# Layer 0 scan: the rows of step sizes, B and C projected half a channel set at a time, in two slots

## The chip, the cores and the metric

The kernel runs on one core of one Trainium2 chip. The metric is the device time of one execution in microseconds (us); lower is better. The kernel is one program for a network of four layers; the change is in the selective scan of layer 0.

## The reference, cut to what matters

Layer 0 takes x of shape (4, 48, 48, 128), normalises it, projects it to 256 channels, convolves it 3x3 and applies silu. The result (xc) is scanned in four directions k: by rows, by columns, and both backwards (L = 2304 positions, d = 256 channels, N = 16 states, R = 8 ranks of the step size):

```python
xs = jnp.stack([x0, x1, x0[..., ::-1], x1[..., ::-1]], axis=1)
x_dbl = jnp.einsum('bkdl,kcd->bkcl', xs, x_proj_w)
dts_r, Bs, Cs = (x_dbl[:, :, :R], x_dbl[:, :, R:R + N], x_dbl[:, :, R + N:])
dts = jnp.einsum('bkrl,kdr->bkdl', dts_r, dt_proj_w)
dt = jax.nn.softplus(dts + dt_proj_b[None, :, :, None])
A = -jnp.exp(A_logs).reshape(K, d, N)
def step(h, inp):
    dt_l, u_l, B_l, C_l = inp
    dA = jnp.exp(dt_l[..., None] * A)
    h = h * dA + (dt_l * u_l)[..., None] * B_l[:, :, None, :]
    y = jnp.einsum('bkdn,bkn->bkd', h, C_l)
    return (h, y)
```

`x_dbl` are the "rows": 8 rows of step sizes, 16 of B and 16 of C for each position, 40 in all, each a sum over the 256 channels. Then come a skip term, a norm, a gate and an output projection, and layers 1 to 3 (deformable convolution, linear attention and experts, causal attention and spectral filters), which the change doesn't touch.

## The kernel before, in words

Layer 0 works image by image (a loop of 4). For each image, the scan is cut into 24 chunks g: four directions k = g // 6, six chunks of 384 positions each (RC = 384). Each chunk has 16 slots, one for each state n; the 384 slots of an image are numbered s, so s = 16 g + n. The 256 channels lie in two halves h of 128 partitions. Everything is fp32.

What a slot s does, on five engines that each follow an order written out in the program and meet at semaphores:

- ScalarE makes `decays(s)` (L500): exp(dt * A), one activation for each half, two slots ahead.
- The input dt * u * B comes into PSUM through `make_input(s)` on TensorE. For the states in TURNED (1, 2, 3, 6, 8, 11, 13, 14) ScalarE scales the turned dt * u by B (`turned_input`, L490, three activations, four slots ahead) and TensorE turns it back (L406, six matmuls). For the others VectorE makes a diagonal matrix of B (`diagonal`, L556, two slots ahead) and TensorE multiplies by it (L408, twelve matmul records).
- VectorE scans: `scan(s)` (L579), one instruction over both halves.
- GpSimd carries the last state of the chunk before into a decay buffer (`carry`, L636) and multiplies the states by C (L649, `hC`). The rows of C come there by DMA: SP stores them to a DRAM scratch (`store_C`, L341) and loads each one spread over all partitions (L352).
- TensorE adds the 16 states up in PSUM: `sum_states(s)` (L419, six matmuls), three slots behind.

Next to this, the next chunk's step sizes are prepared ("project"), each piece in a slot of its own: TensorE makes the rows (`rows`, L361) in slot 0, ScalarE copies them from PSUM (`copy_rows`, L460) in slot 1, TensorE projects the step size of half 0 (`delta`, L377) in slot 2, ScalarE makes a softplus of it (`softplus`, L470, L472, L474) in slot 3, VectorE finishes it (`delta`, L549) in slot 4; half 1 follows in slots 5 to 7; then B is turned and copied (slots 8, 9), and dt * u is turned and copied (slots 10 to 13).

At a chunk's end the sum y goes to SBUF. While k is 0 or 1 (forward), ScalarE copies it in slot 3 of the next chunk (`keep_y`, L506); while k is 2 or 3 (backward), VectorE adds it in slot 2 of the next chunk, behind the scan (`add_y`, L586). Both wait for `sum_states` of the old chunk's last state, and `sum_states` of the new chunk's state 0, in slot 3, waits for them.

TensorE's order in a slot is this:

```python
for s in range(NSTEP):
    if s + 1 < NSTEP:
        make_input(s + 1)
    if s >= 3:
        sum_states(s - 3)
    if s // NS + 1 < NCH:
        project(s // NS + 1, s % NS)
```

`rows(g)` is two matmuls, one for each half of the channels, summed in PSUM (`start` at h = 0, `stop` at h = 1); each shows as two records in the trace. Their moving operand is `inputs(g, h)`: for k even a slice of xc with 384 adjacent elements; for k odd the same image read by columns, with a stride.

Of the kernel before, what the change touches and what calls it, by code (L numbers as in the profile page):

```python
# [62 lines left out]
DI, NS, RK, KD = 256, 16, 8, 4  # L63
RC = 384
NRC = L // RC
# [11 lines left out]
def layer0(nc, x_in, w, x_out, c_rows):  # L77
    with ExitStack() as ctx:
        def sb(name, shape, dt=F32):
            return ctx.enter_context(nc.sbuf_tensor("l0_" + name, shape, dt))  # L80
# [3 lines left out]
        ps = w["psum"]  # L84
# [3 lines left out]
        xp_w = sb("xp_w", [P, KD, 2, RK + 2 * NS])  # L88
# [21 lines left out]
        def cut(at, n):  # L110
# [26 lines left out]
        s_id, s_rows, s_lo, s_dtp, s_btp, s_bt, s_sf, s_dt, s_du, s_tp, s_tc = (scan_sem(n) for n in (  # L137
            "ident_laid", "rows_made", "rows_copied", "dt_projected", "B_turned", "B_copied", "softplus_step", "dt_made",
            "dtu_made", "dtu_turned", "dtu_copied"))
# [12 lines left out]
        with nc.Block() as block:  # L152
# [5 lines left out]
            @block.sync  # L158
            def _(sp):
                sp.dma_start(gnx[:], x_in[:, 0:L]).then_inc(s_x, 16)  # L160
                for dst, src in loads:
                    sp.dma_start(dst, src).then_inc(s_w, 16)
# [23 lines left out]
        with nc.Fori(0, NB) as b:  # L186
# [107 lines left out]
            with nc.Block() as block:  # L294

                def chunk(g):

                    k, j = g // NRC, g % NRC
                    col = (NRC - 1 - j) * RC if k >= 2 else j * RC
                    return k, slice(col, col + RC)  # L300

                def inputs(g, h):

                    k, cs = chunk(g)
                    if k % 2 == 0:
                        return xc[:, h, cs]
                    return xc[:, h, :].rearrange("p (y x) -> p x y", y=HH)[:, cs.start // HH:cs.stop // HH, :]
# [6 lines left out]
                work = 7 * BANK  # L314

                def delta_ps(g, h):

                    o = work if g else 2 * BANK * h
                    return ps[:, o:o + RC]

                def turned_dtu_ps(g):

                    return work if g else 4 * BANK
                x2_ps = [ps[:, 2 * BANK * r + X2_AT:2 * BANK * r + X2_AT + RX] for r in range(2)]

                def half(h):

                    return slice(2 + h * (RC + 2), 2 + h * (RC + 2) + RC)
# [24 lines left out]

                @block.tensor
                def _(pe):
                    def rows(g):
                        if g:
                            pe.wait_ge(s_tc, 2 * g)
                        k = g // NRC
                        for h in range(2):  # L360
                            mm = pe.matmul(ps[0:RK + 2 * NS, work:work + RC], xp_w[:, k, h, :], inputs(g, h), start=(h == 0), stop=(h == 1))  # L361
                        mm.then_inc(s_rows, 1)

                    def turn_B(g):
                        if g:
                            pe.wait_ge(s_dt, 2 * g + 2)
                        for t in range(LB):
                            o = work + RC + t * NS
                            mm = pe.transpose(ps[:, o:o + NS], low[0:NS, g % 2, t * P:(t + 1) * P], ident[0:NS, 0:NS])
                        mm.then_inc(s_btp, 1)  # L370

                    def delta(g, h):
                        if h and g:
                            pe.wait_ge(s_dt, 2 * g + 1)
                        else:
                            pe.wait_ge(s_lo, g + 1)
                        pe.matmul(delta_ps(g, h), dtp_w[32:33 + RK, g // NRC, h * P:(h + 1) * P], low[32:33 + RK, g % 2, :],  # L377
                                  start=True, stop=True).then_inc(s_dtp, 1)

                    def turn_dtu(g, part):  # L380
                        if part and g:
                            pe.wait_ge(s_tc, 2 * g + 1)
                        else:
                            pe.wait_ge(s_bt, g + 1)
                            pe.wait_ge(s_du, g + 1)
                        for t in ((0, 1), (2,))[part]:
                            for h in range(2):
                                o = turned_dtu_ps(g) + (t % 2 if g else t) * DI + h * P
                                mm = pe.transpose(ps[:, o:o + P], dtu[:, g % 2, h, t * P:(t + 1) * P], ident[:])
                        mm.then_inc(s_tp, 1)  # L390

                    def make_input(s):
                        n, g = s % NS, s // NS
                        if n == 0:
                            pe.wait_ge(s_tc, 2 * g + 2)
                        if n in TURNED:
                            pe.wait_ge(s_xT, rank[s] + 1)
                        else:
                            pe.wait_ge(s_dg, rank[s] + 1)
                        if s >= 2:  # L400
                            pe.wait_ge(s_scan, s - 1)
                        for h in range(2):
                            for t in range(LB):
                                o = 2 * BANK * (s % 2) + X2_AT + half(h).start + t * P
                                if n in TURNED:
                                    mm = pe.transpose(ps[:, o:o + P], xT[:, rank[s] % 3, t, h * P:(h + 1) * P], ident[:])  # L406
                                else:
                                    mm = pe.matmul(ps[:, o:o + P], dtuT[:, g % 2, t, h * P:(h + 1) * P], diagB[:, rank[s] % 3, t, :],  # L408
                                                   start=True, stop=True)
                        mm.then_inc(s_x2, 1)  # L410

                    def sum_states(s):
                        n, g = s % NS, s // NS
                        pe.wait_ge(s_hc, s + 1)
                        if n == 0 and g:
                            pe.wait_ge(s_ye, g)
                        for t in range(LB):
                            for h in range(2):
                                mm = pe.matmul(y_ps[:, t, h * P:(h + 1) * P], hC[:, s % NHC, h, t * P:(t + 1) * P], ident[:],  # L419
                                               start=(n == 0 and h == 0 and t % 2 == 0), stop=(n == NS - 1), is_transpose=True,  # L420
                                               skip_group_check=True)
                        mm.then_inc(s_y, 1)

                    def project(g, slot):
                        if slot == 0:
                            rows(g)
                        elif slot == 2:
                            delta(g, 0)
                        elif slot == 5:
                            delta(g, 1)  # L430
                        elif slot == 8:
                            turn_B(g)
                        elif slot == 10:
                            turn_dtu(g, 0)
                        elif slot == 12:
                            turn_dtu(g, 1)

                    pe.transpose(ident_ps, ident[:], ident[:]).then_inc(s_id, 1)
                    for slot in range(NS):
                        project(0, slot)  # L440
                    make_input(0)
# [7 lines that stand above are left out]
                    for s in range(NSTEP - 3, NSTEP):  # L449
                        sum_states(s)  # L450

                @block.scalar
                def _(act):
# [52 lines left out]
                        act.activation(yT[:, k, cs.start // P:cs.stop // P, :], y_ps, ACT.Copy).then_inc(s_ye, 1)  # L506

                    def project(g, slot):
                        if slot == 1:
                            copy_rows(g)  # L510
                        elif slot == 3:
                            softplus(g, 0)
                        elif slot == 6:
                            softplus(g, 1)
                        elif slot == 9:
                            copy_B(g)
                        elif slot == 11:
                            copy_dtu(g, 0)
                        elif slot == 13:
                            copy_dtu(g, 1)  # L520
# [12 lines left out]
                    for s in range(NSTEP):  # L533
                        if s + 2 < NSTEP:
                            decays(s + 2)
                        g = s // NS - 1
# [2310 lines left out]
```

## Time and profile before

| | |
|---|---|
| median of 3 runs | 7457.38 us (7455.82 to 7466.65) |
| the profiled execution, its own time | 7461.88 us |
| its span, first to last instruction | 7459.9 us |
| TensorE matmul (PE) busy | 6818.0 us, 91% |
| TensorE weight load (PEld) busy | 5835.0 us, 78% |
| VectorE (DVE) busy | 6015.2 us, 81% |
| ScalarE (ACT) busy | 4738.0 us, 64% |
| GpSimd (POOL) busy | 4602.9 us, 62% |
| scan instructions (L579) | 1536, 1747 ns each |

The span runs from the first to the last instruction; the execution's own time lies around it. Busy shares are means over the whole program. The scan loops of layer 0 are four stretches, one for each image; in the profile's times the second lies between 1040 us and about 1850 us. The timeline merges adjacent instructions of one kind into a row with their count; a bracket at its end gives the idle time of the engine before the row and what ended it. A row without a bracket follows with no idle time worth naming. The time from one row's start to the next row's start is the better measure of what a group of matmuls takes, since the ends of matmuls are modelled and overlap the next.

### The profile page before, as it was taken

What the parts mean: (1) busy time and instruction counts of PE and PEld (TensorE: products, weight loads), DVE (VectorE), ACT (ScalarE), POOL (GpSimd) and SP (SyncE); (2) the same over time, 40 slices, a digit from 0 to 9 for tenths busy, and PEclk for the clock granted to TensorE, in tenths of its full rate; (3) what the DMA queues carried; (4) which work ended last, traced back from release to release, by engine and by line L of the source; (5) the groups of instructions that cost most, each with busy time, mean ns of one, the idle gap of its engine ahead of it and who ended that gap; (6) DMA issues with size and microseconds to landing.
All of it is one profiled execution on the core that took longest, in us unless ns stands there. A gap on an engine that the chain in (4) does not pass through costs nothing. (4 is left out here: it accounts for less than half of the span.)

```text
span 7459.9 us, 178001 instructions
## 1 busy us (share of the span) xinstructions
PE 6818.0 (91%) x63622; PEld 5835.0 (78%) x63622; DVE 6015.2 (81%) x8957; ACT 4738.0 (64%) x10021; POOL 4602.9 (62%) x5010
## 2 busy tenths in 40 slices
PE   8999989999899998999957999888878989989899
PEld 6888768888588885888836878645657989989898
DVE  7999879999799997999945777546667878878787
ACT  6998769997599985999811433216545545545455
POOL 5998749998399882998917766321213545545454
PEclk9999999999899999999969999989999999999999
DMA  2333213332133331333347776300003434444443
GB/s 65 96 96 94 87 53 95 96 96 87 53 96 96 95 88 52 97 95 96 94 132 234 232 203 191 96 6 18 18 19 102 142 119 135 135 126 141 120 138 120
DMA packets 595169, 775.01 MB, mean 104 GB/s; under 512 B 52215, under 2 KB 528408, under 8 KB 592193
## 3 DMA queue, kind: packets, MB, share of 16 engines
q1 hardware_dynamic: 542529, 594.11, 27.1%
q0 software_dynamic: 51840, 169.91, 7.9%
q8 instruction: 542, 8.88, 0.5%
q14 instruction: 258, 2.11, 0.1%
HBM read 730.16 MB, written 33.66 MB: 102 GB/s over the span
## 5 line engine op out<-in xcount | busy, mean ns | idle before, releaser
L579 DVE TENSOR_TENSOR_SCAN l_arena<-l_arena,psum 128x772 f32<-128x772 f32 x1536 | 2641.6, 1747 | 163.3 <-POOL l_arena L649 60.9
L649 POOL TENSOR_TENSOR l_arena<-l_arena 128x768 f32<-128x768 f32 x1536 | 2590.6, 1687 | 4.2 <-issue 1.6
L500 ACT ACTIVATE l_arena<-l_arena,l_A 128x384 f32<-128x384 f32 x3072 | 1668.2, 603 | 16.2 <-DVE l_arena L579 14.0
L408 PE MATMUL psum<-l_arena 128*128 128x128 f32 x9216 | 1213.5, 282 | 102.5 <-DVE l_arena L579 87.7
L408 PEld LDWEIGHTS psum<-l_arena 128*128 128x128 f32 x9216 | 1091.4, 192 | 272.8 <-issue 221.2
L419 PE MATMUL psum<-l_ident,l_arena 128*128 128x128 f32 x9216 | 1255.4, 273 | 4.6 <-POOL l_arena L649 4.6
L419 PEld LDWEIGHTS psum<-l_ident,l_arena 128*128 128x128 f32 x9216 | 1056.7, 142 | 5.6 <-POOL l_arena L649 5.5
L490 ACT ACTIVATE l_arena<-l_arena,l_BT 128x256 f32<-128x256 f32 x2304 | 994.2, 496 | 7.5
L2683 POOL TENSOR_TENSOR st_U<-st_Uc,st_U 128x384 f16<-128x384 f32 x512 | 478.9, 935 | 783.3 <-ACT st_U L2650 783.3
L1211 POOL DMA_INDIRECT l_G<-neighbours,l_idx x648 | 622.3, 960 | 391.0 <-issue 189.8
L406 PE MATMUL psum<-l_ident,l_arena 128*128 128x128 f32 x4608 | 638.7, 275 | 3.6 <-DVE l_arena L579 2.4
L406 PEld LDWEIGHTS psum<-l_ident,l_arena 128*128 128x128 f32 x4608 | 520.0, 142 | 106.6 <-issue 94.3
L2475 PE MATMUL psum<-st_FS,st_xt 128*128 128x128 f16 x6912 | 518.9, 219 | 9.0 <-DMA st_FS<-filter_sums 8.5
L2500 PE MATMUL psum<-st_U,st_W 128*128 128x128 f16 (+3 forms) x6144 | 509.8, 226 | 11.4 <-ACT st_U L2650 9.6
L1054 DVE TENSOR_TENSOR l_G<-l_G,psum 128x1536 f32<-128x1536 f32 (+1 forms) x144 | 366.3, 2547 | 124.7 <-DMA l_G<-neighbours,l_idx 124.2
L2475 PEld LDWEIGHTS psum<-st_FS,st_xt 128*128 128x128 f16 x6912 | 421.1, 97 | 9.9 <-DMA st_FS<-filter_sums 9.3
L2465 PE MATMUL psum<-st_F,st_xt 128*128 128x128 f16 x4608 | 427.7, 219 | 0.0
L2500 PEld LDWEIGHTS psum<-st_U,st_W 128*128 128x128 f16 x6144 | 403.2, 97 | 14.0 <-ACT st_U L2650 10.5
L556 DVE TENSOR_TENSOR l_arena<-psum,l_BT 128x384 f32<-128x384 f32 x768 | 411.3, 536 | 0.0
L2650 ACT ACTIVATE st_U<-st_Uc 128x384 f16<-128x384 f32 x512 | 266.6, 521 | 223.3 <-DVE st_Uc L2607 211.8
L636 POOL COPY l_arena<-l_arena 128x2 f32<-128x2 f32 x1280 | 240.5, 188 | 243.0 <-DVE l_arena L579 151.4
L1259 PE MATMUL psum<-l_ident,l_G 128*128 128x128 f32 x2592 | 319.6, 284 | 66.5 <-DVE l_G L1054 38.9
(469 smaller groups left out, 11778.4 us busy)
## 6 DMA issues: line engine op xcount, KB each, us to landing
l_arena<-c_rows SPq DMA_DIRECT2D x1536, 192.0 KB, 3.0
st_FS<-filter_sums SPq DMA_DIRECT2D x128, 1155.0 KB, 9.5
st_F<-filter_parts SPq DMA_DIRECT2D x128, 320.5 KB, 7.0
neighbours<-l_xt SPq DMA_DIRECT2D x256, 72.0 KB
st_mab<-in_st_mp SPq DMA_DIRECT2D x68, 256.0 KB, 9.5
st_mab<-in_st_mm SPq DMA_DIRECT2D x68, 256.0 KB, 6.9
l_G<-neighbours,l_idx POOLq DMA_INDIRECT x648
l_arena<-in_x SPq DMA_DIRECT2D x4, 1152.0 KB, 5.3
```

The lines of the kernel that those rows point to most:

```text
L406: mm = pe.transpose(ps[:, o:o + P], xT[:, rank[s] % 3, t, h * P:(h + 1) * P], ident[:])
L408: mm = pe.matmul(ps[:, o:o + P], dtuT[:, g % 2, t, h * P:(h + 1) * P], diagB[:, rank[s] % 3, t, :], start=True, stop=True)
L419: mm = pe.matmul(y_ps[:, t, h * P:(h + 1) * P], hC[:, s % NHC, h, t * P:(t + 1) * P], ident[:], start=(n == 0 and h == 0 and t % 2 == 0), ...
L490: ins = act.activation(xT[:, i % 3, t, :], dtuT[:, g % 2, t, :], ACT.Copy, scale=BT[:, g % 2, t, n:n + 1])
L500: act.activation(decay[:, s % NDC, half(h)], dtv[:, g % 2, h, :], ACT.Exp, scale=A[:, g // NRC, h, n:n + 1]).then_inc(s_exp, 1)
L579: dve.tensor_tensor_scan(hbuf[:, n, run], decay[:, s % NDC, run], x2_ps[s % 2][:, run], 0.0, ALU.mult, ALU.add).then_inc(s_scan, 1)
L649: pool.tensor_tensor(hC[:, s % NHC], halves(hbuf[:, s % NS, :]), Cs[:, s % NCS, :].unsqueeze(1).broadcast_to([P, 2, RC]), ALU.mult).then_i ...
L1211: pool.indirect_dma_start(out=G[:, g, 4 * k:4 * k + 4, :].rearrange("p q c -> p (q c)"), out_offset=None, in_=tables[b], in_offset=bass.In ...
L2465: mm = pe.matmul(ps[:, LOW + i * P:LOW + (i + 1) * P], xt[:, xpart, blk, :], tap[:, r, fpart, z, shift + at:shift + at + P], start=(n + m ...
L2475: mm = pe.matmul(ps[:, at + i * P:at + (i + 1) * P], xt[:, xpart, x0 + LB - 1 - i, :], FS[:, r, fpart, z, three, shift + i * P:shift + (i ...
L2500: mm = pe.matmul(ps[:, o:o + hi - lo], W16[:, r, wpart, z, m, :], U16[:, c, upart, lo - c * RC:hi - c * RC], start=False, stop=False, skip ...
L2683: pool.tensor_tensor(U16[:, c, 1, :], src, U16[:, c, 0, :], ALU.subtract).then_inc(s_ul, 1)
```

## The change

The two matmuls of `rows` are no longer issued together in slot 0. Half h = 0 stays in slot 0, half h = 1 goes to slot 1, and the semaphore that tells of the rows is raised by the second. The copy on ScalarE goes from slot 1 to slot 2. The wait ahead of the rows stays with half 0. Everything else is as it was. For the first chunk of an image, which is projected before the loop, the order of the matmuls is unchanged.

```diff
-                    def rows(g):
-                        if g:
+                    def rows(g, h):
+                        if h == 0 and g:
                             pe.wait_ge(s_tc, 2 * g)
-                        k = g // NRC
-                        for h in range(2):
-                            mm = pe.matmul(ps[0:RK + 2 * NS, work:work + RC], xp_w[:, k, h, :], inputs(g, h), start=(h == 0), stop=(h == 1))
-                        mm.then_inc(s_rows, 1)
+                        mm = pe.matmul(ps[0:RK + 2 * NS, work:work + RC], xp_w[:, g // NRC, h, :], inputs(g, h), start=(h == 0), stop=(h == 1))
+                        if h == 1:
+                            mm.then_inc(s_rows, 1)
...
                     def project(g, slot):
-                        if slot == 0:
-                            rows(g)
+                        if slot < 2:
+                            rows(g, slot)
                         elif slot == 2:
                             delta(g, 0)
...
                     def project(g, slot):
-                        if slot == 1:
+                        if slot == 2:
                             copy_rows(g)
                         elif slot == 3:
                             softplus(g, 0)
```

TensorE's order around slot 0 of a chunk, before: the rows (L361, both halves) stand between the sums of slot 0 and the input of scan 2 (L406).

```order
L408 MATMUL psum<-l_arena 128x128 x6
L419 MATMUL psum<-l_ident,l_arena 128x128 x6
L406 MATMUL psum<-l_ident,l_arena 128x128 x6
L419 MATMUL psum<-l_ident,l_arena 128x128 x6
L361 MATMUL psum<-l_xc,l_xp_w 40x384 x2
L406 MATMUL psum<-l_ident,l_arena 128x128 x6
L419 MATMUL psum<-l_ident,l_arena 128x128 x6
L406 MATMUL psum<-l_ident,l_arena 128x128 x6
L419 MATMUL psum<-l_ident,l_arena 128x128 x6
L377 MATMUL psum<-l_arena,l_dtp_w 128x384
L408 MATMUL psum<-l_arena 128x128 x6
```

The same place with the change, where lines from L361 on have moved up by one or two (L405 is the old L406, L407 the old L408, L418 the old L419, L376 the old L377):

```order
L407 MATMUL psum<-l_arena 128x128 x6
L418 MATMUL psum<-l_ident,l_arena 128x128 x6
L405 MATMUL psum<-l_ident,l_arena 128x128 x6
L418 MATMUL psum<-l_ident,l_arena 128x128 x6
L359 MATMUL psum<-l_xc,l_xp_w 40x384
L405 MATMUL psum<-l_ident,l_arena 128x128 x6
L418 MATMUL psum<-l_ident,l_arena 128x128 x6
L359 MATMUL psum<-l_xc,l_xp_w 40x384
L405 MATMUL psum<-l_ident,l_arena 128x128 x6
L418 MATMUL psum<-l_ident,l_arena 128x128 x6
L376 MATMUL psum<-l_arena,l_dtp_w 128x384
L407 MATMUL psum<-l_arena 128x128 x6
```

The second half of the rows now stands behind the input of scan 2 and the sums of slot 1; the delta and the input of scan 4 stand behind both halves, as before.

ScalarE's order in slots 1 to 3, before: the copy (L460) stands ahead of the decays of scan 4 (L500 x2).

```order
L500 ACTIVATE l_arena<-l_arena,l_A 128x384 x4
L460 ACTIVATE l_arena<-psum 40x384
L500 ACTIVATE l_arena<-l_arena,l_A 128x384 x2
L490 ACTIVATE l_arena<-l_arena,l_BT 128x256 x3
L500 ACTIVATE l_arena<-l_arena,l_A 128x384 x2
L506 ACTIVATE l_yT<-psum 128x768
L470 ACTIVATE l_arena<-psum 128x384
```

With the change:

```order
L499 ACTIVATE l_arena<-l_arena,l_A 128x384 x6
L459 ACTIVATE l_arena<-psum 40x384
L489 ACTIVATE l_arena<-l_arena,l_BT 128x256 x3
L499 ACTIVATE l_arena<-l_arena,l_A 128x384 x2
L505 ACTIVATE l_yT<-psum 128x768
L469 ACTIVATE l_arena<-psum 128x384
```

The copy (now L459) stands behind one more pair of decays, which has joined the four ahead of it, and in front of the same turned input, decays, copy of y and softplus.

## Rows read from the trace of the kernel before

**Rows 1.** Busy time of each engine in the second image's scan loop.

```profile
1075.00:1850.00 775.00, 748.04 (x5884) 652.61 (x5884) 730.80 (x614) 695.25 (x1503) 699.91 (x780) 1.00 0.33 94
```

**Rows 2.** Waits, whole run: waiting engine, line, releaser; us, times, longest.

```profile
ACT l_arena L460 <- PE psum L361: 145.2, 92, 2.2
```

**Rows 3.** Timeline of TensorE, a forward chunk with strided rows: start us, us.

```profile
1305.67 0.82 PE L406 MATMUL psum<-l_ident,l_arena 128*128 128x128 f32 x6
1306.33 0.82 PE L419 MATMUL psum<-l_ident,l_arena 128*128 128x128 f32 x6
1307.07 2.75 PE L361 MATMUL psum<-l_xc,l_xp_w 128*40 128x384 f32 x4
1309.75 0.87 PE L406 MATMUL psum<-l_ident,l_arena 128*128 128x128 f32 x6
1310.46 0.82 PE L419 MATMUL psum<-l_ident,l_arena 128*128 128x128 f32 x6
1311.12 0.82 PE L406 MATMUL psum<-l_ident,l_arena 128*128 128x128 f32 x6
1311.77 0.82 PE L419 MATMUL psum<-l_ident,l_arena 128*128 128x128 f32 x6
1312.52 0.91 PE L377 MATMUL psum<-l_arena,l_dtp_w 9*128 9x384 f32 x2
1313.36 1.60 PE L408 MATMUL psum<-l_arena 128*128 128x128 f32 x12
1314.80 0.82 PE L419 MATMUL psum<-l_ident,l_arena 128*128 128x128 f32 x6
```

**Rows 4.** Timeline of TensorE's weight loads, the same chunk, L361.

```profile
1307.72 0.13 PEld L361 LDWEIGHTS psum<-l_xc,l_xp_w 128*40 128x40 f32 x1 [0.49 <-issue]
1308.36 0.13 PEld L361 LDWEIGHTS psum<-l_xc,l_xp_w 128*40 128x40 f32 x1 [0.51 <-issue]
```

**Rows 5.** Timeline of VectorE, the same chunk, scans 0 and 1, 2, 4.

```profile
1305.38 3.41 DVE L579 TENSOR_TENSOR_SCAN l_arena<-l_arena,psum 128x772 f32<-128x772 f32 x2 [0.28 <-PE psum L408]
...
1310.83 1.76 DVE L579 TENSOR_TENSOR_SCAN l_arena<-l_arena,psum 128x772 f32<-128x772 f32 x1 [1.58 <-PE psum L406]
...
1315.17 1.76 DVE L579 TENSOR_TENSOR_SCAN l_arena<-l_arena,psum 128x772 f32<-128x772 f32 x1 [0.46 <-PE psum L408]
```

**Rows 6.** Timeline of TensorE, a chunk whose next reads xc in order.

```profile
1105.55 0.82 PE L419 MATMUL psum<-l_ident,l_arena 128*128 128x128 f32 x6
1106.30 1.48 PE L361 MATMUL psum<-l_xc,l_xp_w 128*40 128x384 f32 x4
1107.71 0.88 PE L406 MATMUL psum<-l_ident,l_arena 128*128 128x128 f32 x6
```

**Rows 7.** Timeline of TensorE's weight loads, that chunk, L361.

```profile
1106.65 0.12 PEld L361 LDWEIGHTS psum<-l_xc,l_xp_w 128*40 128x40 f32 x1 [0.21 <-issue]
1106.97 0.12 PEld L361 LDWEIGHTS psum<-l_xc,l_xp_w 128*40 128x40 f32 x1 [0.20 <-issue]
```

**Rows 8.** Timeline of VectorE, that chunk, scan 2.

```profile
1108.79 1.76 DVE L579 TENSOR_TENSOR_SCAN l_arena<-l_arena,psum 128x772 f32<-128x772 f32 x1 [0.32 <-PE psum L406]
```

**Rows 9.** Timeline of all engines, a backward strided chunk.

```profile
1715.91 1.76 DVE L579 TENSOR_TENSOR_SCAN l_arena<-l_arena,psum 128x772 f32<-128x772 f32 x1 [1.58 <-PE psum L406]
...
1716.85 0.82 PE L419 MATMUL psum<-l_ident,l_arena 128*128 128x128 f32 x6
...
1717.71 0.95 DVE L586 TENSOR_TENSOR l_yT<-l_yT,psum 128x768 f32<-128x768 f32 x1
```

**Rows 10.** Timeline of ScalarE, the chunk of rows 3.

```profile
1309.86 0.48 ACT L460 ACTIVATE l_arena<-psum 40x384 f32<-40x384 f32 x1 [2.16 <-PE psum L361]
...
1311.26 1.29 ACT L490 ACTIVATE l_arena<-l_arena,l_BT 128x256 f32<-128x256 f32 x3
...
1313.46 0.80 ACT L506 ACTIVATE l_yT<-psum 128x768 f32<-128x768 f32 x1
```

**Rows 11.** Timeline of SP's queue, the same chunk: the store of C rows.

```profile
1311.52 0.38 SPq L341 DMA_DIRECT2D c_rows<-l_arena  x1
```

## The prediction

> **What bounds the kernel now.** I read the busy time of a stretch first, then the table of waits, then the timeline of TensorE, VectorE and ScalarE around slot 0 of a chunk. In 775 us of the second image every engine is busy nine tenths of the time, TensorE most (748.04 us), then VectorE (730.80 us), at a granted clock of 1.00, its 2.4 GHz level [rows 1]. So no engine has much room, and the question is who waits for whom, slot by slot.
>
> The table of waits makes the edit look good: ScalarE's copy (L460) waited 145.2 us, 92 times, for the rows' matmuls (L361) [rows 2]. VectorE waits too. In the chunk at 1305 us the fp32 rows occupy TensorE from 1307.07 to 1309.75 [rows 3], the next make_input (L406, for scan 2) comes behind them, and VectorE stands still for 1.58 us before scan 2 [rows 5]. This is a chunk whose next chunk reads xc by columns (a strided operand). Where the next chunk reads it in order, the rows take 1.41 us [rows 6] and the idle time is 0.32 us [rows 8]. Of the 23 chunks of an image in which rows are projected, the first has no sums to make in its first slots, so TensorE isn't full there; of the other 22, 12 are strided and 10 in order: 48 and 40 over four images.
>
> The decisive reading is the next step. From 1305.67 to the end of L408 at 1314.96 TensorE's rows have no idle time between them at all: sums, inputs, rows, inputs, sums, delta, input of scan 4 [rows 3]. And scan 4, at 1315.17, waits another 0.46 us for exactly that L408 [rows 5]. Its end plus 0.21 us is the scan's start, as at scan 2 (1310.62 and 1310.83). So in a forward chunk **TensorE's queue holds VectorE at slot 4**, whatever happened at slot 2. In a backward chunk it holds it one place earlier: add_y (L586) starts at 1717.71, 0.04 us after the sum of the chunk before (L419) ends at 1717.67, while VectorE would have been free at about 1717.59, when scan 2 (started 1715.91, 1.68 us to the next start) was over [rows 9].
>
> **The change, part by part.** It adds and removes no instruction, no wait and no DMA. It moves one of the two rows matmuls behind make_input(2) and sum_states(-2), and the copy behind one pair of decays.
>
> *The move itself.* Between slot 0 and slot 4 TensorE executes the same work. L408 of slot 4 stays behind both halves, and so does the sum for which add_y waits. What scan 2 gains is waited for at scan 4, or at add_y. For a strided chunk: the first half takes 2 x 0.645 us (1307.72 to 1308.36 and on, record to record, [rows 4]) and its exit 0.10, so L406 starts at 1307.07 + 1.39 = 1308.46 instead of 1309.75, ends at 1309.33, and scan 2 starts at 1309.54. VectorE was ready at 1309.25, so 0.29 of the 1.58 us stay. Scan 3 needs its L406, which starts no earlier than now (1311.12) and ends at 1311.99; scan 4 needs L408 and can't be before 1315.17. Net: 0.
>
> *Two new edges.* The rows have a weight tile of 40 columns between tiles of 128, and that costs at each end. Six matmuls of L419 take 0.66 us from start to start where L406 follows (1310.46 to 1311.12), and 0.74 where L361 follows (1306.33 to 1307.07): 0.08 to 0.09 to enter. The rows take 2.68 us against 4 x 0.645 = 2.58: 0.10 to leave. The L406 behind them takes 0.71 us to the next start against 0.65 (1311.12 to 1311.77): 0.06 more. That is 0.25 us for one excursion to the rows, strided [rows 3, 4]. In order: 0.75 against 0.66 to enter, 1.41 against 4 x 0.32 = 1.28, and the same 0.06 behind: 0.28 us [rows 6, 7]. Before there was one excursion in a chunk, now there are two. Bounds for the second: from below 0, since a change from L419 to L406 costs nothing (0.66 for six), and not less, since no instruction goes. From above 0.36: the other excursion in these rows, the delta with its 9-row weights, costs 0.09 to 0.10 to enter and 0.20 to leave (0.84 to the next start against 2 x 0.32), and 0.06 for the group behind is added. I take 0.25 and 0.28, because the edges that come into being (L419 to L361, L361 to L406) are those of these rows, in this very place.
>
> A rule of the Trainium skill speaks for the lower bound: "TensorE: Matmul & The Clock Gate", Part 2, step by step, says that the load of the next weights is pulled ahead of matmuls in flight. By it the second excursion would be free and the time unchanged. The trace agrees inside the 128-column groups, and not at the edge to the rows.
>
> *Does the edge reach the end?* Yes: TensorE's stretch is full and VectorE waits at its end, so 0.25 us there is 0.25 us at scan 4 or add_y. Behind that VectorE has no idle time until the next TensorE-bound place, which starts from its own scans; nothing takes it back. In the first chunk of an image TensorE has gaps and I count 0. Sum: 48 x 0.25 + 40 x 0.28 = 12.0 + 11.2 = **23.2 us slower**.
>
> *The copy, one slot later.* The second half ends about 1.55 us later than the rows did (0.10 + 0.71 + 0.74), so the copy starts at 1311.4 instead of 1309.86 and ends at 1311.9. TensorE's delta (L377), which waits for it, comes at 1312.52 + 0.25: 0.9 us to spare. ScalarE does the pair of decays, 1.0 us of the 1.40 between 1309.86 and 1311.26, inside its old wait, so all behind it slips by 1.55 - 1.0 = 0.55 us: keep_y ends at 1314.8 instead of 1314.26, and sum_states(0), which waits for it, is due at 1314.80 + 0.25 = 1315.05 [rows 3, 10]. That is 0.2 us to spare. I cost it at nothing; if the cover is gone, TensorE has until L408 for scan 5. On SP's queue the store of the C rows waits for the copy: issued at 1311.52 now, it would go at about 1311.9 [rows 11]. What it stores is first read a whole chunk of slots later. Free.
>
> The profiled execution took 7461.88 us around its span of 7459.9; with 23.2 it would be 7485.1. Its time is 4.5 us above the median of the three runs, 7457.38, so for the median I say 7457.4 + 23.2 = **7481 us**, 0.31% more.
>
> **The rivals.**
> (a) *The wait at scan 2 is what counts, and it goes: faster.* Place: slot 2 of 88 chunks. Price: 40 x 0.32 + 48 x (1.58 - 0.29) = 12.8 + 61.9 = 74.7 us, 7383 us. For it: VectorE is the engine with the scans, and two idle times name L406. It decides from the point at which TensorE, after the rows, has 0.3 us (in order) or 1.3 us (strided) of slack before slot 4. Against: TensorE's rows show none [rows 3], and scan 4 waits 0.46 us now. 6 in 100.
> (b) *The second excursion is free: no change,* 7457 us. It decides if the first L361 of the second block gets its weights in time. The rule of the Trainium skill on loads pulled ahead, in the page named above, stands for this. For it also: L419 to L406 is free. Against: both edges cost 0.08 us or more wherever the rows stand in the trace. 13 in 100.
> (c) *ScalarE becomes late: slower still.* If keep_y ends over 0.2 us later than worked out, sum_states(0) waits, and with it the input of scan 5. 12 chunks of an image keep y this way: 48 x 0.3 us = 14 us on top, 7495 us. Against: L408 of slot 5 has some room of its own in these chunks. 5 in 100.
>
> **How the numbers follow.** Forecast 76 in 100, its own range 7469 to 7489: from half the sum (12 us) to 88 x 0.36 (32 us). A measurement here tells 0.2%, 15 us, from no change. Slower by over that: nearly all of the forecast, and (c): 0.79. Within: (b) and some of the forecast's low end: 0.15. Faster: (a), 0.06. The range 7464 to 7490 holds the forecast with its bounds and leaves out most of (a), (b) and (c).
>
> **What the profile would show.** Right: the idle time before scan 2 gone in chunks in order and near 0.3 us in strided ones; before scan 4 grown from 0.46 to about 1.2 us (strided) with a new one of about 0.7 us before scan 3; a new idle time of about 1.6 us before L586 in strided backward chunks; two blocks of L361 with 0.74 us from the sums to each; TensorE without idle time to L408 of slot 4; a chunk 0.25 us longer; ScalarE's wait before the copy still there, longer: 1311.4 less the old busy end (1307.70) and the pair of decays, 2.7 us in place of 2.16. Wrong: scan 4 earlier relative to scan 0 than 9.79 us (a), the same (b), or an idle time of TensorE before L419 of slot 3 (c).

## The result and the profile after

| | before | after |
|---|---|---|
| median, 12 runs each | 7456.85 us | 7475.85 us |
| ratio, 95% interval | | 1.0022, 1.0013 to 1.0030 |
| span of the profiled execution | 7459.9 us | 7472.6 us |
| scan loop, second image | 804.2 us | 809.8 us |

The kernel became slower: by 19.0 us in the medians, by 16 us (10 to 22) in the ratio. The scan loop, where the change lies, is 5.6 us longer in the second image, 22 us over four. It is measured from the start of the first scan to the start of the last:

```profile
L578 DVE TENSOR_TENSOR_SCAN l_arena<-l_arena,psum x384: 1733/1751/1764, 1041.6 to 1851.4; 128x772 f32<-128x772 f32 x192
```

That is the row of the scan's line in the kernel after, restricted to the second image: shortest, median and longest duration in ns, then first and last start. The same row of before reads 1039.8 to 1844.0. The loop repeats to 0.1 us between executions with the same order, so it is the sharper measure of the two. What lies outside the four loops is the same program in every kernel here, but for small fills ahead of the loops in the kernels with wide or deep weights, and its sum moved between 4225.5 and 4245.1 us from one profiled execution to another. In the two compared here it was 4242.8 us before and 4233.4 after, which is why the loops' 22 us stand beside 12.7 us in the two spans.

The chunk of rows 3 to 5, now. TensorE's timeline (start us, us):

```profile
1309.97 0.82 PE L418 MATMUL psum<-l_ident,l_arena 128*128 128x128 f32 x6
1310.72 1.46 PE L359 MATMUL psum<-l_xc,l_xp_w 128*40 128x384 f32 x2
1312.11 0.87 PE L405 MATMUL psum<-l_ident,l_arena 128*128 128x128 f32 x6
1312.82 0.82 PE L418 MATMUL psum<-l_ident,l_arena 128*128 128x128 f32 x6
1313.57 1.46 PE L359 MATMUL psum<-l_xc,l_xp_w 128*40 128x384 f32 x2
1314.96 0.87 PE L405 MATMUL psum<-l_ident,l_arena 128*128 128x128 f32 x6
1315.67 0.82 PE L418 MATMUL psum<-l_ident,l_arena 128*128 128x128 f32 x6
1316.42 0.91 PE L376 MATMUL psum<-l_arena,l_dtp_w 9*128 9x384 f32 x2
1317.25 1.60 PE L407 MATMUL psum<-l_arena 128*128 128x128 f32 x12
1318.69 0.82 PE L418 MATMUL psum<-l_ident,l_arena 128*128 128x128 f32 x6
```

VectorE's, scans 0 and 1, 2, 3, 4:

```profile
1309.03 3.41 DVE L578 TENSOR_TENSOR_SCAN l_arena<-l_arena,psum 128x772 f32<-128x772 f32 x2 [0.27 <-PE psum L407]
...
1313.19 1.76 DVE L578 TENSOR_TENSOR_SCAN l_arena<-l_arena,psum 128x772 f32<-128x772 f32 x1 [0.30 <-POOL l_arena L635]
...
1316.03 1.76 DVE L578 TENSOR_TENSOR_SCAN l_arena<-l_arena,psum 128x772 f32<-128x772 f32 x1 [0.64 <-PE psum L405]
1319.06 1.76 DVE L578 TENSOR_TENSOR_SCAN l_arena<-l_arena,psum 128x772 f32<-128x772 f32 x1 [1.27 <-PE psum L407]
```

Before, from the last sums ahead of the rows to L408 of slot 4 took 1306.33 to 1313.36, 7.03 us [rows 3]. Now it takes 1309.97 to 1317.25, 7.28 us. TensorE has no idle time in either. Scan 2 comes 1.29 us earlier after scan 0 than before (4.16 us in place of 5.45), and scan 4 comes 0.24 us later (10.03 in place of 9.79 [rows 5]). The idle time of 1.58 + 0.46 us became 0.30 + 0.64 + 1.27: moved to a later slot, and longer. The releaser that the row of scan 2 names, POOL L635, made the copy for scan 2 at 1309.36, long before (the one at 1312.90 is for scan 4, by the program's order); the scan started 0.21 us after L405's end at 1312.98, the same distance as before.

In a backward strided chunk the wait went to add_y:

```profile
1721.44 1.76 DVE L578 TENSOR_TENSOR_SCAN l_arena<-l_arena,psum 128x772 f32<-128x772 f32 x1 [0.30 <-POOL l_arena L635]
1724.78 0.95 DVE L585 TENSOR_TENSOR l_yT<-l_yT,psum 128x768 f32<-128x768 f32 x1 [1.58 <-PE psum L418]
```

Over the image the groups of VectorE's lines say the same (busy us, mean ns, then idle us before them and its releasers). Before:

```profile
L579 DVE TENSOR_TENSOR_SCAN l_arena<-l_arena,psum 128x772 f32<-128x772 f32 x384 | 660.4, 1747 | 40.8 <-POOL l_arena L649 15.0 <-PE psum L408 14.5 <-PE psum L406 10.2
...
L586 DVE TENSOR_TENSOR l_yT<-l_yT,psum 128x768 f32<-128x768 f32 x12 | 11.4, 950 | 3.1 <-PE psum L419 2.7
```

After:

```profile
L578 DVE TENSOR_TENSOR_SCAN l_arena<-l_arena,psum 128x772 f32<-128x772 f32 x384 | 660.7, 1749 | 34.8 <-PE psum L407 23.0 <-PE psum L405 5.6 <-POOL l_arena L648 3.5
...
L585 DVE TENSOR_TENSOR l_yT<-l_yT,psum 128x768 f32<-128x768 f32 x12 | 11.4, 952 | 14.7 <-PE psum L418 14.7
```

The idle time before scans was 40.8 us and is 34.8, before add_y it was 3.1 and is 14.7. Together it grew by 5.6 us, which is the loop's growth.

And ScalarE's copy in the chunk above, and the copy of y behind it. The rows end about 1.55 us later than before, and the decays of scan 4, done ahead of the copy, fill only some 1.0 us of that, so the copy waits longer (2.70 us in place of 2.16 [rows 10]):

```profile
1315.06 0.48 ACT L459 ACTIVATE l_arena<-psum 40x384 f32<-40x384 f32 x1 [2.70 <-PE psum L359]
...
1317.66 0.79 ACT L505 ACTIVATE l_yT<-psum 128x768 f32<-128x768 f32 x1
```

The copy of y ends at 1318.45, and the sums of state 0 (L418), which wait for it, start at 1318.69. That is 1.44 us behind L407, as before (1313.36 to 1314.80 [rows 3]), so ScalarE held nothing up.

### The profile page after: what moved, and what is told of

The parts are those of the page before. It is cut to its first block and busy times, and to the rows that moved or that the text cites. A ratio compares the mean times of both kernels' runs of the same rounds, so it can differ in the third digit from the quotient of the medians.

```text
span 7472.6 us, 177997 instructions
## 1 busy us (share of the span) xinstructions
PE 6826.9 (91%) x63618; PEld 5815.5 (78%) x63622; DVE 6016.8 (81%) x8957; ACT 4737.7 (63%) x10021; POOL 4607.7 (62%) x5010
## 5 line engine op out<-in xcount | busy, mean ns | idle before, releaser
L407 PE MATMUL psum<-l_arena 128*128 128x128 f32 x9216 | 1213.5, 282 | 100.8 <-DVE l_arena L578 86.1
L407 PEld LDWEIGHTS psum<-l_arena 128*128 128x128 f32 x9216 | 1091.5, 192 | 271.0 <-issue 243.4
L418 PE MATMUL psum<-l_ident,l_arena 128*128 128x128 f32 x9216 | 1255.4, 273 | 4.6 <-POOL l_arena L648 4.6
L418 PEld LDWEIGHTS psum<-l_ident,l_arena 128*128 128x128 f32 x9216 | 1056.7, 142 | 5.6 <-POOL l_arena L648 5.5
L405 PEld LDWEIGHTS psum<-l_ident,l_arena 128*128 128x128 f32 x4608 | 515.8, 142 | 192.2 <-issue 176.5
L405 PE MATMUL psum<-l_ident,l_arena 128*128 128x128 f32 x4608 | 644.3, 276 | 1.8 <-DVE l_arena L578 0.7
L635 POOL COPY l_arena<-l_arena 128x2 f32<-128x2 f32 x1280 | 245.7, 192 | 261.1 <-DVE l_arena L578 250.6
```

## The experiments

Two questions were open: whether it is really the edges that cost and not the move or the copy, and what an edge is. Eight more kernels were run. The loop is that of the second image throughout; the other three images agree within 0.1 us, except in the kernel with the rows in slot 1. Each ratio is to runs of before made in the same session (their medians were 7456.85, 7458.90 and 7453.67 us in the three sessions), so the ratios and the loops compare from row to row, and the medians only roughly.

| kernel | rows weights | loop us | median us | ratio to before, 95% interval |
|---|---|---|---|---|
| before | 40 columns | 804.2 | 7456.85 | |
| after | 40, in slots 0 and 1 | 809.8 | 7475.85 | 1.0022 (1.0013 to 1.0030) |
| copy late | 40, slot 0 | 804.2 | 7457.83 | 1.0000 (0.9991 to 1.0010) |
| rows in slot 1 | 40, slot 1 | 813.2 | 7485.30 | 1.0038 (1.0024 to 1.0052) |
| three parts | 40, three places | 815.8 | 7496.03 | 1.0052 (1.0035 to 1.0069) |
| wide split | 128, in slots 0 and 1 | 799.4 | 7434.32 | 0.9968 (0.9957 to 0.9978) |
| wide whole | 128, slot 0 | 798.9 | 7433.98 | 0.9971 (0.9961 to 0.9981) |
| short strides | 40, slot 0 | 789.2 | 7393.95 | 0.9918 (0.9901 to 0.9934) |
| wide whole, deep delta | 128, slot 0 | 794.2 | 7417.31 | 0.9949 (0.9933 to 0.9966) |
| all three | 128, slot 0 | 778.8 | 7353.75 | 0.9868 (0.9852 to 0.9885) |

### The copy alone

```diff
                     def project(g, slot):
-                        if slot == 1:
+                        if slot == 2:
                             copy_rows(g)
```

> The kernel before with one part of the change alone: the copy of the rows goes from slot 1 to slot 2, both rows matmuls stay in slot 0. Theory 1 (the new edges on TensorE cost everything, the copy nothing): TensorE's order is that of before, so the scan loop of an image (first scan to last scan) stays at 804.3 us, and the time within 5 us of before (7457). Theory 2 (the late copy costs: ScalarE or a wait for the copy): the loop grows toward the 809.8 us of the changed kernel, the time by up to 19 us.

```profile
L579 DVE TENSOR_TENSOR_SCAN l_arena<-l_arena,psum x384: 1732/1751/1762, 1038.4 to 1842.6; 128x772 f32<-128x772 f32 x192
```

804.2 us, ratio 1.0000. With the rows where they were, the late copy costs nothing, and theory 2 falls. Rival (c) needs later rows as well, which this kernel doesn't have; it is answered by the trace of the kernel after, where the copy of y still ended 0.24 us before the sums that wait for it.

### The rows together in slot 1

```diff
                     def project(g, slot):
-                        if slot == 0:
+                        if slot == 1:
                             rows(g)
...
-                        if slot == 1:
+                        if slot == 2:
                             copy_rows(g)
```

> Both rows matmuls together in slot 1, behind the input of scan 2 and the sums of slot 1, the copy in slot 2: the whole move, but one excursion to the 40-column weights as before. Theory 1 (TensorE is full from slot 0 to slot 4, so a move inside it gains nothing, and only the second excursion costs): the idle time before scan 2 is gone, scan 4 starts 9.79 us after scan 0 (strided, forward) as before, the loop stays at 804.3 us, the time at that of before within 5 us. Theory 2 (what scan 2 gains can be kept): the loop shrinks, up to 18 us an image. Theory 3 (the later rows cost by themselves): the loop grows as with the change, to 809.8 us.

This one missed: I expected 804.3 us, and it took 813.2 (811.7 in the first and the third image, 813.2 and 813.1 in the second and the fourth). The 1.5 us between the images come from their first chunk and from the clock. TensorE still has idle time there. In the second image the granted clock stood at 0.50, its 1.2 GHz level, until about 1052 us, and the rows took 2.58 us to the next start; in the first image it was at 1.00 from about 93 us, before the rows, and they took 1.42. The figure to explain is therefore 811.7. TensorE's timeline in the strided forward chunk:

```profile
1316.88 0.82 PE L419 MATMUL psum<-l_ident,l_arena 128*128 128x128 f32 x6
1317.84 0.85 PE L406 MATMUL psum<-l_ident,l_arena 128*128 128x128 f32 x6
1318.53 0.82 PE L419 MATMUL psum<-l_ident,l_arena 128*128 128x128 f32 x6
1319.28 2.75 PE L361 MATMUL psum<-l_xc,l_xp_w 128*40 128x384 f32 x4
```

From L419 to L406 it takes 0.96 us where 0.66 is the usual step. In this kernel scan 0 started at 1315.93 and ended at 1317.69, and the input of scan 2 goes where the data of scan 0 lay in PSUM, so the program makes L406 wait for that end (`pe.wait_ge(s_scan, s - 1)` in `make_input`). Without rows in front of it TensorE comes there 0.3 us early and stands. 20 of the 22 chunks became 0.33 to 0.35 us longer (22 x 0.34 = 7.5 us, against the loop's 7.4 in the first image). So the rows in slot 0 have a use: they cover that wait. The first half alone covers it as well (0.77 us to the next start in order, 1.39 strided): TensorE has no idle time behind it in the kernel after, which is why the change doesn't pay for that wait. Theory 2 is out, since no gain at scan 2 was kept. Theory 1 holds only with this addition: a move inside the full stretch gains nothing, and it can lose.

### One more cut

```diff
-                        mm = pe.matmul(ps[0:RK + 2 * NS, work:work + RC], xp_w[:, g // NRC, h, :], inputs(g, h), start=(h == 0), stop=(h == 1))
+                        if h == 0:
+                            pe.matmul(ps[0:RK + 2 * NS, work:work + RC], xp_w[:, g // NRC, h, :], inputs(g, h), start=True, stop=False)
+                        else:
+                            rows_part(g, 1)
...
+                        mm = pe.matmul(ps[0:RK + 2 * NS, work + 192 * q:work + 192 * q + 192], xp_w[:, g // NRC, 1, :], src, start=False, stop=(q == 1))
...
                             make_input(s + 1)
+                        if s % NS == 1 and s // NS + 1 < NCH:
+                            rows_part(s // NS + 1, 0)
                         if s >= 3:
                             sum_states(s - 3)
```

> The changed kernel with the second half's matmul cut once more, into 192 and 192 positions, with the sums of slot 1 between the two: three excursions to the 40-column weights in a chunk in place of two, the same columns streamed. Theory 1 (an excursion costs 0.25 to 0.28 us and reaches the end): the loop grows by 88/4 x 0.25 to 0.28 = 5.5 to 6.2 us an image, from 809.8 to 815.3 to 816.0, the time by 22 to 25 us over the changed kernel. Theory 2 (the loss of the change comes from elsewhere, its copy or its waits): the loop stays at 809.8 us.

```profile
L590 DVE TENSOR_TENSOR_SCAN l_arena<-l_arena,psum x384: 1732/1750/1764, 1050.3 to 1866.1; 128x772 f32<-128x772 f32 x192
```

815.8 us: 6.0 more than after, inside the 5.5 to 6.2 expected; over the four loops it is 23.8 us. The medians differ by 20.2 us, a little under the 22 to 25 expected, but they are of two sessions. The cost goes with the number of excursions.

### Wide weights, split and whole

The rows' weights are read 128 columns wide. The further 88 columns are the neighbouring weights (and zeros at the end); their outputs go to PSUM partitions that nobody reads. The output's first 40 rows are the same.

```diff
-        xp_w = sb("xp_w", [P, KD, 2, RK + 2 * NS])
+        xp_all = sb("xp_w", [P, KD * 2 * (RK + 2 * NS) + P - RK - 2 * NS])
+        xp_w = xp_all[:, 0:KD * 2 * (RK + 2 * NS)].rearrange("p (k h r) -> p k h r", k=KD, h=2)
+
+        def xp_tile(k, h):
+            o = (2 * k + h) * (RK + 2 * NS)
+            return xp_all[:, o:o + P]
...
+                dve.memset(xp_all[:, KD * 2 * (RK + 2 * NS):], 0.0)
...
-                        mm = pe.matmul(ps[0:RK + 2 * NS, work:work + RC], xp_w[:, g // NRC, h, :], inputs(g, h), start=(h == 0), stop=(h == 1))
+                        mm = pe.matmul(ps[:, work:work + RC], xp_tile(g // NRC, h), inputs(g, h), start=(h == 0), stop=(h == 1))
```

> The changed kernel with rows weights read 128 columns wide (the 88 further columns are neighbouring weights, their outputs are not used), so that no weight tile of another width stands between the sums and the inputs. Theory 1 (the edge is the change of the tile's width, at which the next weights are not loaded ahead): both excursions lose 0.25 to 0.28 us, the loop goes from 809.8 to about 798 us an image, the time to about 7430. Theory 2 (the edge comes with the rows' long moving operand or their own reads, not with the width): the loop stays at 809.8 us, or grows a little since 128 columns load more slowly than 40.

> The kernel before (both rows matmuls in slot 0) with the rows weights read 128 columns wide. Theory (an edge costs because of the tile's width): one excursion of 0.25 us (strided) or 0.28 us (in order) goes, so the loop shrinks from 804.3 by 12 x 0.25 + 10 x 0.28 = 5.8 to 798.5 us an image, and the time by 23 us. If with wide weights the split costs nothing and gains nothing, the wide split kernel (799.4 us a loop) and this one are within about 1 us of each other. Rival (the split gains once its edges are free): the wide split kernel's loop is clearly the shorter.

The split kernel's loop went from 809.8 to 799.4 us (798 expected), the whole one's from 804.2 to 798.9 (798.5 expected). First the weight loads of the split kernel after this edit, in the strided chunk, then its matmuls:

```profile
1296.17 0.69 PEld L425 LDWEIGHTS psum<-l_ident,l_arena 128*128 128x128 f32 x6
1296.83 0.30 PEld L366 LDWEIGHTS psum<-l_xc,l_xp_w 128*128 128x128 f32 x2
1297.57 0.16 PEld L412 LDWEIGHTS psum<-l_ident,l_arena 128*128 128x128 f32 x1 [0.43 <-issue]
```

```profile
1296.28 0.82 PE L425 MATMUL psum<-l_ident,l_arena 128*128 128x128 f32 x6
1296.94 1.45 PE L366 MATMUL psum<-l_xc,l_xp_w 128*128 128x384 f32 x2
1298.21 0.83 PE L412 MATMUL psum<-l_ident,l_arena 128*128 128x128 f32 x6
1298.88 0.82 PE L425 MATMUL psum<-l_ident,l_arena 128*128 128x128 f32 x6
1299.53 1.45 PE L366 MATMUL psum<-l_xc,l_xp_w 128*128 128x384 f32 x2
```

The load for L366 starts at 1296.83, 0.11 us before its matmul, and the load for the first L412 at 1297.57, 0.64 before its own: one matmul ahead. In the kernel after, they came together with their matmuls, at both edges:

```profile
1313.57 0.15 PEld L359 LDWEIGHTS psum<-l_xc,l_xp_w 128*40 128x40 f32 x2 [0.17 <-issue]
1314.95 0.14 PEld L405 LDWEIGHTS psum<-l_ident,l_arena 128*128 128x128 f32 x1 [1.24 <-issue]
```

Entering takes nothing now (0.66 to the next start), half the rows 1.27 to 1.28 in place of 1.39, and L412 behind them 0.67 in place of 0.71. The excursion is nearly free, and the split and the whole kernel differ by 0.5 us a loop. So the split by itself gains nothing once its edges cost next to nothing: that is what was left of rival (a).

A load ahead of the matmuls in flight is what the Trainium skill describes ("TensorE: Matmul & The Clock Gate", Part 2, step by step). In these traces it happens between tiles of 128 by 128, and not when the tile goes from 128 to 40 columns or back. It isn't the narrow tile as such: inside the block of 40-column tiles the loads did go ahead. The last load of the strided rows started at 1308.36 [rows 4], 0.64 us before its matmul, the fourth record, at 1309.00. What costs is the change of shape.

### Short strides

Only for the rows of chunks read by columns, in the kernel before:

```diff
-                            mm = pe.matmul(ps[0:RK + 2 * NS, work:work + RC], xp_w[:, k, h, :], inputs(g, h), start=(h == 0), stop=(h == 1))
+                            out, src = rows_io(g, h, RK + 2 * NS)
+                            mm = pe.matmul(out, xp_w[:, k, h, :], src, start=(h == 0), stop=(h == 1))
                         mm.then_inc(s_rows, 1)
+
+                    def rows_io(g, h, m):
+                        out = ps[0:m, work:work + RC]
+                        if g // NRC % 2 == 0:
+                            return out, inputs(g, h)
+                        return out.rearrange("p (x y) -> p y x", y=HH), inputs(g, h).rearrange("p x y -> p y x")
```

> The kernel before; where the next chunk is read by columns (k odd), the rows matmuls stream the same 384 positions in the order y, then 8 adjacent x, and write to PSUM with the stride instead. Theory 1 (the strided chunks' rows take 2.68 us in place of 1.41 because each element of the moving operand is 192 bytes from the last, and TensorE is full there): the rows take about 1.4 us everywhere, a strided chunk becomes as long as one in order, and the loop shrinks by 12 x 1.26 = 15.1 to 789 us. Theory 2 (the stride in the output or the short runs of 8 cost the same): the loop stays at 804.3 us.

```profile
1285.83 1.48 PE L362 MATMUL psum<-l_xc,l_xp_w 128*40 128x384 f32 x4
1287.25 0.88 PE L413 MATMUL psum<-l_ident,l_arena 128*128 128x128 f32 x6
```

A strided chunk's rows now take 1.42 us, as in order, and the loop is 789.2 us (789 expected). The stride in the output costs nothing here. This kernel takes TensorE's work out of the stretch in which the change only moved it, and the time follows: 12 x 1.26 = 15.1 us expected, 15.0 measured.

### The delta's weights as deep as the others

On top of the wide whole kernel: zeros around the 9 rows of the step sizes' weights, and a finite constant in the rows of the copied buffer that nothing else fills, so that the product is the same. The load of these weights waits for the zeros.

```diff
-        dtp_w = sb("dtp_w", [64, KD, DI])
+        dtp_w = sb("dtp_w", [P, KD, DI])
...
+                pool.memset(dtp_w[:], 0.0).then_inc(s_dz, 1)
...
                 dve.memset(low[32:64], 1.0)
+                dve.memset(low[64:128], 1.0)
...
-                        pe.matmul(delta_ps(g, h), dtp_w[32:33 + RK, g // NRC, h * P:(h + 1) * P], low[32:33 + RK, g % 2, :],
+                        pe.matmul(delta_ps(g, h), dtp_w[:, g // NRC, h * P:(h + 1) * P], low[:, g % 2, :],
```

> The wide whole kernel, with the step-size matmuls (delta, L377 of before) given weights of 128 rows too, zero outside their 9, and the 128 rows of the copied rows' buffer as the other operand. Theory (each change of the weight tile's shape costs, and what lies in slots 0 to 4 reaches the end): the excursion to the 9-row weights in slot 2 (0.10 to enter, 0.20 to leave) goes, the loop shrinks by another 22 x 0.25 to 0.3 = 5.5 to 6.6 us from the wide whole kernel's, to about 792 us. Rival (the width in columns matters, the rows don't): the loop stays at the wide whole kernel's.

```profile
1296.50 0.82 PE L431 MATMUL psum<-l_ident,l_arena 128*128 128x128 f32 x6
1297.15 0.81 PE L389 MATMUL psum<-l_arena,l_dtp_w 128*128 128x384 f32 x2
1297.80 1.50 PE L420 MATMUL psum<-l_arena 128*128 128x128 f32 x12
```

L431 to L389 0.65 us (0.75 before), L389 to L420 0.65 (0.84 before [rows 3]): the 9-row tile had edges too. The loop shrank by 4.7 us where I expected 5.5 to 6.6. I had counted all 22 chunks, though the sum for which add_y waits stands ahead of the delta; in backward chunks the delta isn't on the path. Chunk by chunk, the twelve forward ones give 4.5 us (nine of them 0.39 each) and the ten backward ones 0.2 together. The 0.39 are all there at scan 4: 0.10 to enter, 0.19 to leave, and 0.10 because the L420 block behind the delta now ends 1.50 us after its start and not 1.60. I had left the last part out.

### All three

> Wide rows weights, deep delta weights and short strides together, rows whole in slot 0. If each saving stays on the path to the end: 804.3 - 15.1 - 5.8 - 6 = 777 us a loop. VectorE had 0.32 + 0.46 us idle before scans 2 and 4 in a forward chunk in order and less in a backward one, so some of it is not to be had there: 777 to 780 us a loop, 7350 to 7365 us in all. Rival (TensorE is not what holds the loop): no shorter than the kernel with the short strides alone.

The edit is the sum of the last three. 778.8 us a loop (777 to 780 expected), 7353.75 us, 0.9868 of before with an interval of 0.9852 to 0.9885. It is faster than the kernel before and the kernel after. VectorE, in the same strided chunk:

```profile
1268.21 3.41 DVE L598 TENSOR_TENSOR_SCAN l_arena<-l_arena,psum 128x772 f32<-128x772 f32 x2 [0.27 <-PE psum L427]
...
1272.12 1.76 DVE L598 TENSOR_TENSOR_SCAN l_arena<-l_arena,psum 128x772 f32<-128x772 f32 x1
...
1274.25 3.58 DVE L598 TENSOR_TENSOR_SCAN l_arena<-l_arena,psum 128x772 f32<-128x772 f32 x2
```

The idle time before scans 2 and 4 is gone, and VectorE is now the busiest engine (it still waits 0.27 us for TensorE before scan 0). In 740 us of this kernel's second loop it is busy 724.64 us and TensorE 710.12:

```profile
1040.00:1780.00 740.00, 710.12 (x5830) 654.87 (x5829) 724.64 (x609) 695.24 (x1509) 693.44 (x776) 1.00 0.34 99
```

## Why the prediction was right

- **TensorE is full from slot 0 to slot 4, so the move gains nothing.** Right: no idle time in the rows after, and scan 4 didn't come earlier. Taking work out of the stretch (short strides) gave its full length.
- **A second excursion costs 0.25 us strided, 0.28 in order.** Right: 7.28 against 7.03 us in the stretch, strided, and 5.6 us a loop where 12 x 0.25 + 10 x 0.28 = 5.8 was the sum. From chunk to chunk, 21 of the 22 grew by 0.25 to 0.28 us, and the first chunk of the image not at all, as predicted. The missing 0.2 us is one strided backward chunk, the last but one of an image in which rows are projected: before, it took 34.77 us where its neighbours take 34.56, and after it takes 34.81 like them, so it grew by 0.04. Why it was longer before is open. A third excursion cost 6.0 us a loop more. All the parts of the price came from edges that already stood in the rows of before. Rival (b), free loads, fell at these edges; loads went ahead as it says as soon as the tile had 128 columns.
- **Scan 2 starts 4.16 us after scan 0 with 0.29 us idle.** It did, with 0.30. The waits that would grow did so: 0.64 us before scan 3 (0.7 predicted), 1.27 before scan 4 (1.2), 1.58 before add_y (1.6), 2.70 before the copy (2.7).
- **The copy is free, with 0.2 us to spare before sum_states(0).** The copy alone left the loop unchanged, and with the later rows 0.24 us were left. Rival (c) fell by the second of these, in the trace of the kernel after.
- **The total.** 22.2 us over four loops against 23.2 predicted. The medians say 19.0 us and the ratio 10 to 22: the loops' number lies at the interval's upper end. The loops' 22.2 us are 0.30% and the forecast was 0.31%; the ratio says 0.22%. The rest of the program differs by up to 20 us between single executions, and whether it explains the difference isn't shown.
- **"Between slot 0 and slot 4 TensorE executes the same work. Net: 0."** Right for this change, but as a rule too simple. It took for granted that TensorE never waits in the stretch, whatever the order. The rows in slot 1 showed a wait (L406 for the end of scan 0) that the rows' first half happens to cover. The prediction didn't see that cover of 0.3 us, so that its "Net: 0" held for this change was in part luck.

## What to carry to other kernels

An idle time in front of an instruction is worth something only if the next place doesn't wait for the same queue: follow the full engine on to the next wait before crediting the gain. Interleaving adds edges, and on TensorE an edge between weight tiles of different shape has a price of its own; giving a small tile the size of its neighbours, with zeros or with outputs that nobody reads, took it away here. Before moving an instruction out of a slot, ask which wait it has been covering.

## What the runs showed of the hardware that I had not expected

- A weight tile of 40 columns between tiles of 128 cost 0.25 to 0.28 us each time, and one of 9 rows instead of 128 cost 0.39 up to the next scan, though their loads took less time: 0.11 to 0.13 us a load against 0.19 to 0.21 for the same weights read 128 columns wide, and 0.18 against 0.19 with 9 rows. With 128 by 128 tiles throughout, the loads went ahead of the matmuls again and the step fell to the plain one (0.65 to 0.67 us for a group of six).
- An fp32 matmul whose moving operand steps 192 bytes between elements took 0.645 us for a record of 384, and 0.32 us with runs of 8 adjacent elements, as with 384 adjacent ones. A write to PSUM with a step of 192 bytes cost nothing (1.42 us for the four records against 1.41). Which length of run begins to help was not tried.
